# Grouped attention: the rotation's half swap as a stream shuffle on VectorE, and the row maximum split into two f32r parts

## The chip, the cores and the metric

The program runs on one core of one Trainium2 chip. The metric is the device time of one execution in microseconds (us), the median of several. In the names of the profile PE is TensorE, PEld its weight loads, DVE VectorE, ACT ScalarE, POOL GpSimd, and SP the engine whose queue issues most DMAs.

## The reference, cut to what matters

A decoder of two layers in six stages, each followed by a layer norm: grouped attention, cross attention, a gated feed forward part with attention, squared attention, another cross attention, and a mixture of experts. The change is in the first stage alone, which has 16 sequences of 128 tokens, model width 512, 32 query heads and 8 key heads of width 16:

```
q = (x @ Wq), k = (x @ Wk), v = (x @ Wv), by heads of 16 channels
rope(x) = [x1 * cos - x2 * sin, x2 * cos + x1 * sin]     # x1, x2: the two halves of a head's 16 channels
scores = q k^T / 4, causal; attn = softmax(scores); out = (attn v) Wo + b; x = layernorm(x + out)
```

The same stage of the kernel also computes what the second stage needs: its rotated queries (from the new x), its rotated keys and its values (from ctx).

## The kernel before, in words

`grouped_attention` (from line 1224) works on 16 batches b. Queries and keys are made for four batches at a time as 5 blocks of 128 channels by 512 tokens (`project(k)`, 12 f32r matmuls: three products of high and low parts, line 1470). Seven blocks are made ahead of the loop over b (`project` 0 to 6, with `project_v(0)` after block 4); the loop makes one block per batch for b + 1 = 1, 2, 3, 5, 6, 7, 9, 10, 11, two for b + 1 = 4 and 8, and none from 12 on (`blocks_of`). In three batches it also makes values (`project_v`). Beside them the loop makes one key tile (`project_key(b)`), one value tile (`project_next_v(b)`) and, from b = 2, one query tile (`project_query(b - 2)`) of the next stage.

Every tile that is rotated, 20 blocks, 16 keys and 16 queries, goes the same way. ACT copies it from PSUM to one of three buffers `raw` (`take`, lines 1691 to 1696). POOL multiplies it by the cosine (`times_cos`). PE multiplies it by a permutation matrix that swaps the halves of each head (`turn`, line 1508, f32, 128x128 by 128x512) into the PSUM tile `turn_ps`. DVE multiplies that by the sine (`times_sin`, lines 1804 and 1809). POOL adds both products (`rotate`, line 1963).

The softmax is computed on transposed scores, so the row maximum has to be turned first. For batch b the order on PE is: `scores(b, 0)`, `scores(b, 1)` (a mask matmul in bf16 and the score matmuls in f32 over four row groups), DVE's `row_max` of each half, `transpose_max(b)` (line 1553), then DVE's `split_max(b)`: the negated maximum is written to SBUF (line 1832) and cut into three bf16 parts in five instructions (lines 1832 to 1840). SP's `send_max(b)` sends the parts in three DMAs to rows of `m_row`, which has two buffers. PE goes on with `scores_t(b, 0)`, which may overwrite the PSUM tile of the turned maximum once line 1832 has read it, then `project_key(b)`, `turn` of a query, `project_next_v(b)`, and `add_max(b, 0)` (line 1575: four bf16 matmuls of 3 rows, each in its row group, which add the maximum to the scores). After that come `project_o(b - 1, 0)` (line 1607), `scores_t(b, 1)`, `add_max(b, 1)`, `project_o(b - 1, 1)`, the blocks, `scores(b + 1, ...)`, `values(b)`, `sums(b)` and so on. ACT takes the exponentials after each `add_max`.

Each engine runs its own list in the order written, and waits on semaphores that count the steps of the others. DVE's order in batch b is `normalize(b - 1)` (a reciprocal of 128x512, line 1847, and a product, line 1852), `add_v_bias(b)`, sine of a query, `residual`, `moments`, `row_max(b + 1, 0)`, `finish_norm`, sine of a key, sines of blocks but the last, `row_max(b + 1, 1)`, sine of the last block, `split_max(b + 1)`. The stages are separated by a barrier of all engines.

Of the kernel before, what the change touches and what calls it, by code (L numbers as in the profile page):

```python
# [12 lines left out]
P = 128  # L13
# [1210 lines left out]
def grouped_attention(nc, tag, x_in, x_t_in, x_out, wq_d, wk_d, wv_d, wo_d, bo_d, perm_d, cos_d, sin_d, parity_d,  # L1224
# [7 lines left out]
    AT_FIRST = BLOCKS + 2  # L1232
    with Phase(nc) as ph:
# [7 lines left out]
        perm = sb(f"{tag}_perm", [P, P])  # L1241
# [9 lines left out]
        ones_bf = sb(f"{tag}_ones_bf", [P, P], BF16)  # L1251
# [11 lines left out]
        m_neg = sb(f"{tag}_m_neg", [KV * I, P])  # L1263
        m_rest = sb(f"{tag}_m_rest", [KV * I, P])
        m_parts = sb(f"{tag}_m_parts", [KV * I, 3, P], BF16)
        m_row = sb(f"{tag}_m_row", [P, 2, 2, N], BF16)
# [23 lines left out]
        turn_ps = ph.ps(f"{tag}_turn", [P, N])  # L1290
# [13 lines left out]
        names = ("zeroed set_done w_hi_done w_lo_done x_hi_done x_lo_first x_lo_done qk_full raw_done turn_full cos_done "  # L1304
# [3 lines left out]
        (zeroed, set_done, w_hi_done, w_lo_done, x_hi_done, x_lo_first, x_lo_done, qk_full, raw_done, turn_full, cos_done,  # L1308
# [4 lines left out]
        consts = [(perm, perm_d), (cos, cos_d[:, KEY]), (sin, sin_d[:, KEY]), (parity, parity_d), (ident, ident_d),  # L1313
# [46 lines left out]
        with nc.Block() as block:  # L1360
            @block.sync
            def _(sp):
# [12 lines left out]
                def send_max(b):  # L1375
                    sp.wait_ge(m_step, 5 * (b + 1))
                    if b >= 2:
                        sp.wait_ge(st_full, 8 * (b - 1))
                    for p in range(3):
                        sp.dma_start(m_row[p:P:32, b % 2, :, :].rearrange("j h t -> j (h t)"), m_parts[:, p, :]  # L1380
                                     ).then_inc(m_ld, 16)
# [65 lines left out]
            def _(pe):  # L1447
# [107 lines left out]
                def scores_t(b, half):  # L1555

                    for j in range(4):
                        if half == 1:
                            pe.wait_ge(exp_done, 8 * b + j + 1)
                        elif j == 0:  # L1560
                            pe.wait_ge(m_step, 5 * b + 1)
                        nc.tensor.matmul(sc_ps[:, j, :].rearrange("p (i s) -> p i s", i=4), ident_bf[:, :],
                                         mask_t[:, :].rearrange("p (o s) -> p o s", o=1).to_broadcast([P, 4, P]),
                                         start=True, stop=False, skip_group_check=True)
                    for j in range(4):
                        r = slice(32 * j, 32 * j + 32)
# [46 lines left out]
                for k in range(1, BLOCKS):  # L1613
                    project(k)
                    turn(0, k - 1)
                project_v(0)
                turn(0, BLOCKS - 1)
# [5 lines left out]
                turn(0, first)  # L1623
                project(second)
                transpose_max(0)
                turn(0, second)

                for b in range(B):
# [3 lines left out]
                    if b >= 3:  # L1632
                        turn(1, b - 3)
# [15 lines left out]
                    turn(2, b)  # L1649
                    for k in blocks[-1:]:  # L1650
                        project(k)
                    for k in blocks[:-1]:
                        turn(0, k)
# [3 lines left out]
                    for k in blocks[-1:]:  # L1657
                        turn(0, k)
# [4 lines left out]
                turn(1, B - 3)  # L1663
# [3 lines left out]
                turn(1, B - 2)  # L1667
                project_query(B - 1)
                turn(1, B - 1)

            @block.scalar
            def _(act):
# [109 lines left out]
            def _(dve):  # L1782
                nc.vector.memset(ones_bf[:, :], 1.0).then_inc(set_done, 1)
# [14 lines left out]
                def times_sin(kind, n):  # L1798
                    s = at(kind, n)
                    dve.wait_ge(turn_full, s + 1)  # L1800
                    if s >= 2:
                        dve.wait_ge(rope_done, s - 1)
                    if kind == 0:
                        nc.vector.tensor_tensor(turned_s[:, s % 2, :].rearrange("p (n t) -> p n t", n=4),
                                                turn_ps[:, :].rearrange("p (n t) -> p n t", n=4),
                                                sin[:, :].rearrange("p (o t) -> p o t", o=1).to_broadcast([P, 4, P]),
                                                ALU.mult).then_inc(sin_done, 1)
# [20 lines left out]
                def split_max(b):  # L1828
                    dve.wait_ge(mT_full, b + 1)
                    if b > 0:  # L1830
                        dve.wait_ge(m_ld, 48 * b)
                    nc.vector.tensor_scalar(m_neg[:, :], sc_ps[0:KV * I, 0, 0:P], -1.0, None, ALU.mult).then_inc(m_step, 1)
                    dve.wait_ge(m_step, b * 5 + 1)
                    nc.vector.tensor_copy(m_parts[:, 0, :], m_neg[:, :]).then_inc(m_step, 1)
                    dve.wait_ge(m_step, b * 5 + 2)
                    nc.vector.tensor_tensor(m_rest[:, :], m_neg[:, :], m_parts[:, 0, :], ALU.subtract).then_inc(m_step, 1)
                    dve.wait_ge(m_step, b * 5 + 3)
                    nc.vector.tensor_copy(m_parts[:, 1, :], m_rest[:, :]).then_inc(m_step, 1)
                    dve.wait_ge(m_step, b * 5 + 4)
                    nc.vector.tensor_tensor(m_parts[:, 2, :], m_rest[:, :], m_parts[:, 1, :], ALU.subtract  # L1840
                                            ).then_inc(m_step, 1)
# [2077 lines left out]
def decoder(nc, i, out):  # L3919

    def dram(name, shape, dt=F32):
# [8 lines left out]
                      i["rope_perm"], i["a0_cos"], i["a0_sin"], i["a0_parity"], i["ident"], i["half"], i["ident_bf"],  # L3930
# [122 lines left out]
```

## Time and profile before

| | |
|---|---|
| median of 3 runs | 3454.83 us (3448.98 to 3464.68) |
| the profiled execution | 3458.54 us, its span 3456.8 us |
| mean granted TensorE clock | 0.939 of full speed |
| PE busy | 3040.2 us (88%) |
| DVE busy | 2114.3 us (61%) |
| first stage | from 0 to about 510.7 us of the span |

The span runs from the first to the last instruction of the profiled execution. "busy" is the time in which the engine had an instruction in work. PE's matmuls are pipelined and their ends are modelled, so that what a matmul takes from PE is read from the start of the next one, not from its own length. A bracket behind a row of the timeline is the idle time before it, and what ended it.

### The profile page before, as it was taken

The numbers are of one execution on the slowest core, as the hardware profiler recorded it, in microseconds if no ns is written. First come the engines' busy times: TensorE is split into PE (matmuls) and PEld (weight loads), VectorE is DVE, ScalarE is ACT, GpSimd is POOL, SyncE is SP. The second block draws the span as 40 slices with busy tenths as digits, with TensorE's granted clock in tenths as the row PEclk, the third lists the DMA queues.
The fourth block names the chain that finished last, engine by engine and source line by source line (L and its number), as shares of the span: only waits on it lengthen the run. The fifth ranks groups of instructions, "written<-read, shape, count | busy, mean of one in ns | idle before, by whom it ended". The sixth has DMA issues, their size and how long they took to land. (4 is left out here: it accounts for less than half of the span.)

```text
span 3456.8 us, 57813 instructions
## 1 busy us (share of the span) xinstructions
PE 3040.2 (88%) x21948; PEld 1766.5 (51%) x21948; DVE 2114.3 (61%) x2636; ACT 1531.2 (44%) x2642; POOL 938.5 (27%) x1397
## 2 busy tenths in 40 slices
PE   7999968999669968999996999599999995889997
PEld 4444323333256646888885676222222223767785
DVE  4555658999335443444444344699999992562167
ACT  3222324777533213333331333179999994321132
POOL 3444451333200001111120245423333331001154
PEclk9999986999879988999998999789999997899998
DMA  3222335555231005455443122323333323339976
GB/s 114 67 73 75 87 96 130 155 157 146 77 107 33 9 26 146 126 160 154 127 152 99 54 89 76 117 72 94 97 99 100 93 81 102 90 113 364 401 244 181
DMA packets 370294, 413.27 MB, mean 120 GB/s; under 512 B 62737, under 2 KB 246673, under 8 KB 368786
## 3 DMA queue, kind: packets, MB, share of 16 engines
q1 hardware_dynamic: 211552, 251.69, 23.6%
q10 hardware_dynamic: 135938, 100.69, 9.5%
q0 software_dynamic: 22528, 57.19, 5.5%
q8 instruction: 175, 2.87, 0.4%
q14 instruction: 101, 0.83, 0.1%
HBM read 299.88 MB, written 108.92 MB: 118 GB/s over the span
## 5 line engine op out<-in xcount | busy, mean ns | idle before, releaser
L394 ACT ACTIVATE c_probs<-c_st 128x512 f32<-128x512 f32 x1536 | 834.7, 597 | 214.9 <-PE c_st L320 202.6
L433 DVE TENSOR_REDUCE c_maxes<-c_s 128x2 f32<-128x1024 f32 x768 | 898.7, 1211 | 27.6 <-PE c_s L301 26.2
L337 PE MATMUL c_o<-c_probs,c_v_aug 128*32 128x256 f32 x6144 | 496.9, 395 | 46.8 <-ACT c_o_raw L404 28.9
L301 PE MATMUL c_s<-c_k_st,c_q_st 48*128 48x512 bf16 (+1 forms) x1536 | 344.8, 446 | 67.8 <-DMA c_k_st<-c_k_dram 40.1
L320 PE MATMUL c_st<-c_q_st,c_k_st 51*128 51x512 bf16 (+1 forms) x1536 | 319.6, 394 | 5.3 <-DVE c_y L459 5.1
L301 PEld LDWEIGHTS c_s<-c_k_st,c_q_st 48*128 48x128 bf16 (+1 forms) x1536 | 100.9, 128 | 401.8 <-issue 226.7
L337 PEld LDWEIGHTS c_o<-c_probs,c_v_aug 128*32 128x32 f32 x6144 | 124.4, 108 | 317.7 <-issue 214.3
L2961 DVE TENSOR_TENSOR f_w_lo<-f_w_raw,f_w_hi 128x1536 fp32r<-128x1536 f32 x64 | 116.8, 1825 | 108.7 <-ACT f_w_hi L2882 108.6
L320 PEld LDWEIGHTS c_st<-c_q_st,c_k_st 51*128 51x128 bf16 (+1 forms) x1536 | 144.0, 127 | 53.7 <-issue 23.0
L2882 ACT ACTIVATE f_w_hi<-f_w_raw 128x1536 fp32r<-128x1536 f32 x64 | 95.3, 1488 | 92.7 <-PE f_out_ps L2832 58.8
L3028 POOL CAST f_parts<-f_ctx 128x512 bf16<-128x512 f32 x16 | 12.4, 775 | 444.7 <-DMA f_ctx<-in_ctx 444.7
L2995 DVE TENSOR_TENSOR f_hidden<-f_gate,f_up_ps 128x512 f32<-128x512 f32 x64 | 43.9, 686 | 135.9 <-PE f_up_ps L2794 106.3
L1824 DVE TENSOR_REDUCE a_maxes<-a_sc 128x4 f32<-128x512 f32 x128 | 79.5, 684 | 73.6 <-PE a_sc L1544 73.6
L2589 POOL TENSOR_TENSOR a_kept<-a_weights,a_keep_t 128x512 f32<-128x512 f32 x64 | 80.4, 1289 | 142.7 <-ACT a_weights L2390 142.7
L605 POOL CAST c_m_parts<-c_m_t 128x64 bf16<-128x64 f32 (+1 forms) x96 | 23.4, 244 | 322.6 <-DVE c_m_t L443 322.6
L1148 DVE TENSOR_REDUCE g_maxes<-g_sc 128x4 f32<-128x512 f32 x64 | 39.7, 682 | 107.0 <-PE g_sc L920 107.0
L3902 POOL DMA_INDIRECT f_early<-x_dram,f_e_token x22 | 20.9, 952 | 301.2 <-PE f_up_ps L3318 211.5
L2918 ACT ACTIVATE f_hidden_hi<-f_hidden 128x512 fp32r<-128x512 f32 x64 | 40.5, 632 | 140.4 <-DVE f_hidden L2995 140.4
L1734 ACT ACTIVATE a_probs<-a_sc 128x512 f32<-128x512 f32 x128 | 66.1, 602 | 82.2 <-PE a_sc L1575 82.2
L2832 PE MATMUL f_out_ps<-f_w_hi,f_hidden_hi 128*128 128x512 f32 x256 | 99.7, 389 | 0.0
L2832 PE MATMUL f_out_ps<-f_w_lo,f_hidden_hi 128*128 128x512 f32 x256 | 99.6, 389 | 0.0
L2832 PE MATMUL f_out_ps<-f_w_hi,f_hidden_lo 128*128 128x512 f32 x256 | 99.6, 389 | 0.0
(419 smaller groups left out, 6017.7 us busy)
## 6 DMA issues: line engine op xcount, KB each, us to landing
f_w_raw<-in_f_win ACTq DMA_DIRECT2D x96, 256.0 KB, 3.1
f_w_raw<-in_f_wup ACTq DMA_DIRECT2D x96, 256.0 KB, 3.4
f_w_raw<-in_f_wdown ACTq DMA_DIRECT2D x96, 256.0 KB, 3.7
c_o_dram<-c_o_raw SPq DMA_DIRECT2D x64, 256.0 KB, 2.5
f_x<-x_dram SPq DMA_DIRECT2D x48, 256.0 KB, 4.3
c_k_dram<-f_parts ACTq DMA_DIRECT2D x96, 128.0 KB, 2.7
c_q_dram<-a_parts SPq DMA_DIRECT2D x96, 128.0 KB, 2.4
c_q_st<-c_q_dram SPq DMA_DIRECT2D x128, 96.0 KB, 2.2
```

The source lines that it names most:

```text
L301: mm = nc.tensor.matmul(s1_ps[:, i, half, :], q_st[r:r + ROWS, s, i, tt * P:(tt + 1) * P], k_st[r:r + ROWS, s, i, :], start=True, stop=True)
L320: nc.tensor.matmul(st_ps[:, st_bank(j, e), :], k_st[r:r + ROWS + MP, s, i, st * P:(st + 1) * P], q_st[r:r + ROWS + MP, s, i, :], start=Tru ...
L337: mm = nc.tensor.matmul(o_ps[32 * h:32 * h + 32, queries], v_aug[:, (j // NG) % NBS, st, head_of(j, h), :], probs[:, (st * 4 + i * 2 + hal ...
L394: nc.scalar.activation(probs[:, e % 8, :], st_ps[:, st_bank(j, e), :], ACT.Exp).then_inc(exp_done, 1)
L433: nc.vector.tensor_reduce(maxes[:, j % 2, :].rearrange("p (h r) -> p h r", h=2)[:, :, i * KT + tt], s1_ps[:, i, :, :], AX.X, ALU.max).then ...
L1734: nc.scalar.activation(probs[:, half, j, :], sc_ps[:, j, :], ACT.Exp).then_inc(exp_done, 1)
L1824: nc.vector.tensor_reduce(out[:, 2 * half:2 * half + 2, :], sc_ps[:, j, :].rearrange("p (i h s) -> p i h s", i=2, h=2), AX.X, ALU.max).the ...
L2589: nc.gpsimd.tensor_tensor(kept[:, b % 2, j, :, :], weights[:, j, :, :], keep_t[:, :].rearrange("p (o s) -> p o s", o=1).to_broadcast([P, D ...
L2832: mm = nc.tensor.matmul(out_ps[:, t, :], a[:, f % 2, tokens], w[:, n % RING, DOWN, :], start=(f == 0 and k == 0), stop=(f == NF - 1 and k ...
L2882: nc.scalar.activation(w_hi[:, n % RING, :, :], w_raw[:, n % 2, :, :], ACT.Copy).then_inc(w_hi_done, 1)
L2961: nc.vector.tensor_tensor(w_lo[:, n % RING, :, :], w_raw[:, n % 2, :, :], w_hi[:, n % RING, :, :], ALU.subtract).then_inc(w_lo_done, 1)
L2995: nc.vector.tensor_tensor(hidden[:, f % 2, :], gate[:, f % 2, :], up_ps[:, f % 2, :], ALU.mult).then_inc(hidden_done, 1)
```

## The change

The rotation: `turn`, its PSUM tile, its semaphore and the permutation matrix (a DMA of 64 KB among the constants) are gone. DVE swaps the halves itself, by a stream shuffle inside each group of 32 partitions, from `raw` to `turned_s`, and multiplies `turned_s` by the sine in place. The wait for the constants moves to PE's list ahead of the first scores. The maximum: two parts in f32r instead of three in bf16, both read from PSUM, so that `split_max` has two instructions; two DMAs instead of three, of twice the bytes each; one buffer of `m_row` instead of two. `scores_t(b, 0)` now waits for both instructions of `split_max`, and the matmuls of `add_max` have two f32r rows. Cut to its core:

```diff
+    SWAP = [c - c % 16 + (c % 16 + 8) % 16 for c in range(32)]
-        m_parts = sb(f"{tag}_m_parts", [KV * I, 3, P], BF16)
-        m_row = sb(f"{tag}_m_row", [P, 2, 2, N], BF16)
+        m_parts = sb(f"{tag}_m_parts", [KV * I, 2, P], F32R)
+        m_row = sb(f"{tag}_m_row", [P, 2, N], F32R)
                 def send_max(b):
-                    sp.wait_ge(m_step, 5 * (b + 1))
-                    if b >= 2:
-                        sp.wait_ge(st_full, 8 * (b - 1))
-                    for p in range(3):
+                    sp.wait_ge(m_step, 2 * (b + 1))
+                    if b > 0:
+                        sp.wait_ge(st_full, 8 * b)
+                    for p in range(2):
...
-                def turn(kind, n):
-                    s = at(kind, n)
-                    pe.wait_ge(raw_done, s + 1)
-                    if s == 0:
-                        pe.wait_ge(const_ld, 16 * NCONST)
-                    else:
-                        pe.wait_ge(sin_done, s)
-                    nc.tensor.matmul(turn_ps[:, :], perm[:, :], raw[:, s % RAWS, :], start=True, stop=True
-                                     ).then_inc(turn_full, 1)
                 def scores_t(b, half):
-                            pe.wait_ge(m_step, 5 * b + 1)
+                            pe.wait_ge(m_step, 2 * (b + 1))
                 def add_max(b, half):
-                        nc.tensor.matmul(sc_ps[:, j, :], ones_bf[32 * j:32 * j + 3, :],
-                                         m_row[32 * j:32 * j + 3, b % 2, half, :],
+                        nc.tensor.matmul(sc_ps[:, j, :], ones_r[32 * j:32 * j + 2, :],
+                                         m_row[32 * j:32 * j + 2, half, :],
...
                 def take(kind, n):
                     if s >= RAWS:
-                        act.wait_ge(turn_full, s - RAWS + 1)
+                        act.wait_ge(swapped, s - RAWS + 1)
                 def times_sin(kind, n):
                     s = at(kind, n)
-                    dve.wait_ge(turn_full, s + 1)
+                    out = turned_s[:, s % 2, :]
+                    dve.wait_ge(raw_done, s + 1)
                     if s >= 2:
                         dve.wait_ge(rope_done, s - 1)
+                    nc.vector.stream_shuffle(out, raw[:, s % RAWS, :], SWAP).then_inc(swapped, 1)
+                    dve.wait_ge(swapped, s + 1)
-                        nc.vector.tensor_tensor(turned_s[:, s % 2, :], turn_ps[:, :], next_sin[:, :], ALU.mult
-                                                ).then_inc(sin_done, 1)
+                        nc.vector.tensor_tensor(out, out, next_sin[:, :], ALU.mult).then_inc(sin_done, 1)
                 def split_max(b):
-                    nc.vector.tensor_scalar(m_neg[:, :], sc_ps[0:KV * I, 0, 0:P], -1.0, None, ALU.mult).then_inc(m_step, 1)
-                    nc.vector.tensor_copy(m_parts[:, 0, :], m_neg[:, :]).then_inc(m_step, 1)
-                    nc.vector.tensor_tensor(m_rest[:, :], m_neg[:, :], m_parts[:, 0, :], ALU.subtract).then_inc(m_step, 1)
-                    nc.vector.tensor_copy(m_parts[:, 1, :], m_rest[:, :]).then_inc(m_step, 1)
-                    nc.vector.tensor_tensor(m_parts[:, 2, :], m_rest[:, :], m_parts[:, 1, :], ALU.subtract
-                                            ).then_inc(m_step, 1)
+                    turned = sc_ps[0:KV * I, 0, 0:P]
+                    nc.vector.tensor_scalar(m_parts[:, 0, :], turned, -1.0, None, ALU.mult).then_inc(m_step, 1)
+                    dve.wait_ge(m_step, b * 2 + 1)
+                    nc.vector.scalar_tensor_tensor(out=m_parts[:, 1, :], in0=turned, scalar=-1.0, in1=m_parts[:, 0, :],
+                                                   op0=ALU.mult, op1=ALU.subtract).then_inc(m_step, 1)
```

All calls of `turn` in PE's list are taken out: four between the first projections, one after `project_v(0)`, two more ahead of the loop, and in each batch one after `values`, one after `project_key` (from b = 3), and one for each block, of which the last stands after `sums`. At the end of the stage there are three more, for the last queries.

## Rows read from the trace of the kernel before

**Rows 1.** Windows over the first stage, then the timeline of PE where the second begins.

```profile
50.30:510.70 460.40, 407.81 (x2302) 177.45 (x2300) 261.01 (x372) 121.65 (x224) 194.33 (x164) 0.96 0.26 76
...
516.81 0.80 PE L301 MATMUL c_s<-c_k_st,c_q_st 48*128 48x512 f32 x2 [19.14 <-DMA c_k_st<-c_k_dram]
```

**Rows 2.** Timeline of PE: batch 7's wait (first row), then batch 8.

```profile
263.74 0.39 PE L1575 MATMUL a_sc<-a_m_row,a_ones_bf 3*128 3x512 bf16 x4 [1.57 <-DMA a_m_row<-a_m_parts]
...
289.71 1.04 PE L1562 MATMUL a_sc<-a_mask_t,a_ident_bf 128*128 128x512 bf16 x4 [0.37 <-DVE a_m_neg L1832]
...
293.65 1.16 PE L1497 MATMUL a_proj<-a_next_wv,a_ctx 128*128 128x128 f32 x8
295.40 0.39 PE L1575 MATMUL a_sc<-a_m_row,a_ones_bf 3*128 3x512 bf16 x4 [0.59 <-DMA a_m_row<-a_m_parts]
296.47 1.98 PE L1607 MATMUL a_misc<-a_wo,a_o_norm 128*128 128x512 f32 x4 [0.68 <-DVE a_o_norm L1852]
...
313.88 1.12 PE L1508 MATMUL a_turn<-a_raw,a_perm 128*128 128x512 f32 x2
314.84 1.02 PE L1490 MATMUL a_proj<-a_x_new,a_next_wq 128*128 128x512 f32 x2
...
316.34 1.04 PE L1562 MATMUL a_sc<-a_mask_t,a_ident_bf 128*128 128x512 bf16 x4 [0.37 <-DVE a_m_neg L1832]
```

**Rows 3.** Timeline of PE: batch 13, which has no block.

```profile
418.73 1.04 PE L1562 MATMUL a_sc<-a_mask_t,a_ident_bf 128*128 128x512 bf16 x4 [0.37 <-DVE a_m_neg L1832]
...
424.80 1.98 PE L1607 MATMUL a_misc<-a_wo,a_o_norm 128*128 128x512 f32 x4 [0.65 <-DVE a_o_norm L1852]
...
434.57 1.12 PE L1508 MATMUL a_turn<-a_raw,a_perm 128*128 128x512 f32 x2
```

**Rows 4.** Timeline of DVE: the end of batch 8; the last row is of batch 13.

```profile
312.18 2.48 DVE L1824 TENSOR_REDUCE a_maxes<-a_sc 128x4 f32<-128x512 f32 x4 [4.08 <-PE a_sc L1544]
315.04 0.69 DVE L1804 TENSOR_TENSOR a_turned_s<-a_turn,a_sin 128x512 f32<-128x512 f32 x1 [0.38 <-PE a_turn L1508]
316.01 0.28 DVE L1832 TENSOR_SCALAR a_m_neg<-a_sc 32x128 f32<-32x128 f32 x1 [0.28 <-PE a_sc L1553]
316.32 0.88 DVE L1834 CAST a_m_parts<-a_m_neg 32x128 bf16<-32x128 f32 x1
317.24 1.25 DVE L1836 TENSOR_TENSOR a_m_rest<-a_m_neg,a_m_parts 32x128 f32<-32x128 f32 x1
...
318.98 3.34 DVE L1847 RECIPROCAL a_recip<-a_misc 128x512 f32<-128x512 f32 x1
...
437.73 2.48 DVE L1824 TENSOR_REDUCE a_maxes<-a_sc 128x4 f32<-128x512 f32 x4 [1.30 <-PE a_sc L1544]
```

**Rows 5.** Single lines of DVE, count, ns least/median/most.

```profile
L1863 DVE BATCH_NORM_STATS2 a_stats<-a_y x16: 694/695/695, 88.6 to 488.9; 128x6 f32<-128x512 f32 x16
...
L1874 DVE TENSOR_SCALAR a_x_new<-a_y,a_mv,a_rstd x16: 534/536/1492, 95.9 to 490.7; 128x512 f32<-128x512 f32 x16
...
L1836 DVE TENSOR_TENSOR a_m_rest<-a_m_neg,a_m_parts x16: 279/1252/1316, 49.5 to 463.6; 32x128 f32<-32x128 f32 x16
```

**Rows 6.** Timeline of PE in the second stage: two f32r matmuls in two row groups.

```profile
700.19 0.40 PE L320 MATMUL c_st<-c_q_st,c_k_st 50*128 50x512 f32 x2
```

**Rows 7.** Timelines of ACT, PE and DVE ahead of the loop.

```profile
26.22 0.60 ACT L1691 ACTIVATE a_raw<-a_proj 128x512 f32<-128x512 f32 x1
...
30.50 3.73 PE L1523 MATMUL a_proj<-a_wv,a_x_t 128*128 128x128 f32 x32
...
39.88 1.19 PE L1470 MATMUL a_proj<-a_x_hi,a_w_hi 128*128 128x512 f32 x4
...
48.82 0.28 DVE L1832 TENSOR_SCALAR a_m_neg<-a_sc 32x128 f32<-32x128 f32 x1 [0.86 <-PE a_sc L1553]
```

**Rows 8.** Windows of the four stretches of the stage at a lower clock.

```profile
199.80:206.65 6.85, 6.61 (x16) 2.38 (x20) 1.38 (x3) 2.17 (x5) 2.51 (x2) 0.53 0.61 170
...
sum 20.52, PE 19.86 PEld 7.19 DVE 4.08 ACT 6.68 POOL 9.03; mean PE 4.97 PEld 1.80 DVE 1.02 ACT 1.67 POOL 2.26
```

More of the change, by code:

```diff
@@ L1250, in grouped_attention @@
         ones_pad = sb(f"{tag}_ones_pad", [P, 2, 32])
-        ones_bf = sb(f"{tag}_ones_bf", [P, P], BF16)
+        ones_r = sb(f"{tag}_ones_r", [P, P], F32R)
         x_t = sb(f"{tag}_x_t", [P, 2, DK, N])
@@ L1303, in grouped_attention @@
         next_v_stored = sem(f"{tag}_next_v_stored")
-        names = ("zeroed set_done w_hi_done w_lo_done x_hi_done x_lo_first x_lo_done qk_full raw_done turn_full cos_done "
+        names = ("zeroed set_done w_hi_done w_lo_done x_hi_done x_lo_first x_lo_done qk_full raw_done swapped cos_done "
                  "sin_done rope_done pad_done v_full v_done s1_full max_done mT_full m_step m_ld st_full exp_done o_full "
@@ L1312, in grouped_attention @@
              sem(f"{tag}_{n}") for n in names]
-        consts = [(perm, perm_d), (cos, cos_d[:, KEY]), (sin, sin_d[:, KEY]), (parity, parity_d), (ident, ident_d),
+        consts = [(cos, cos_d[:, KEY]), (sin, sin_d[:, KEY]), (parity, parity_d), (ident, ident_d),
                   (ident_bf, ident_bf_d), (mask, mask_d), (mask_t, mask_t_d), (minus_half, half_d), (bo, bo_d),
@@ L1375, in send_max @@
                 def send_max(b):
-                    sp.wait_ge(m_step, 5 * (b + 1))
-                    if b >= 2:
-                        sp.wait_ge(st_full, 8 * (b - 1))
-                    for p in range(3):
-                        sp.dma_start(m_row[p:P:32, b % 2, :, :].rearrange("j h t -> j (h t)"), m_parts[:, p, :]
-                                     ).then_inc(m_ld, 16)
+                    sp.wait_ge(m_step, 2 * (b + 1))
+                    if b > 0:
+                        sp.wait_ge(st_full, 8 * b)
+                    for p in range(2):
+                        sp.dma_start(m_row[p:P:32, :, :].rearrange("j h t -> j (h t)").bitcast(F32),
+                                     m_parts[:, p, :].bitcast(F32)).then_inc(m_ld, 16)
                 def store(b):
@@ L1614, in _ @@
                     project(k)
-                    turn(0, k - 1)
                 project_v(0)
-                turn(0, BLOCKS - 1)
+                pe.wait_ge(const_ld, 16 * NCONST)
                 pe.wait_ge(set_done, 5)
@@ L1622, in _ @@
                 scores(0, 1)
-                turn(0, first)
                 project(second)
                 transpose_max(0)
-                turn(0, second)
                 for b in range(B):
@@ L1631, in _ @@
                     project_key(b)
-                    if b >= 3:
-                        turn(1, b - 3)
                     project_next_v(b)
@@ L1648, in _ @@
                     values(b)
-                    turn(2, b)
                     for k in blocks[-1:]:
                         project(k)
-                    for k in blocks[:-1]:
-                        turn(0, k)
                     if b + 1 < B:
@@ L1656, in _ @@
                     sums(b)
-                    for k in blocks[-1:]:
-                        turn(0, k)
                     if b >= 2:
@@ L1662, in _ @@
                         transpose_max(b + 1)
-                turn(1, B - 3)
                 project_query(B - 2)
@@ L1666, in _ @@
                 project_o(B - 1, 1)
-                turn(1, B - 2)
                 project_query(B - 1)
-                turn(1, B - 1)
             @block.scalar
@@ L1782, in _ @@
             def _(dve):
-                nc.vector.memset(ones_bf[:, :], 1.0).then_inc(set_done, 1)
+                nc.vector.memset(ones_r[:, :].bitcast(F32), 1.0).then_inc(set_done, 1)
                 for half in range(2):
@@ L3929, in decoder @@
     grouped_attention(nc, "a0", i["x"], i["x_t"], x1, i["a0_wq"], i["a0_wk"], i["a0_wv"], i["a0_wo"], i["a0_bo"],
-                      i["rope_perm"], i["a0_cos"], i["a0_sin"], i["a0_parity"], i["ident"], i["half"], i["ident_bf"],
+                      i["a0_cos"], i["a0_sin"], i["a0_parity"], i["ident"], i["half"], i["ident_bf"],
                       i["mask"], i["mask_t"], i["ctx"], [i["c0_wq"], i["c0_wk"], i["c0_wv"]], i["c0_bqk"], i["c0_bv"],
@@ L4039 @@
         a[f"c0_{name}"] = np.concatenate([t / 4, t], 1)
-    a["rope_perm"] = np.zeros((P, P), np.float32)
-    a["rope_perm"][c - c % 16 + (c % 16 + 8) % 16, c] = 1
     nc = _bacc.Bacc("TRN2", target_bir_lowering=False, num_devices=1)
```

20 lines of the change are left out of this document (6 added, 14 removed).

## The prediction

> **What bounds the kernel now.** I read the windows first: the loop of the first stage is 460.40 us, PE is busy for 407.81 of them (89%) and DVE for 261.01 (57%) [rows 1]. The second stage's first matmul has waited 19.14 us for data that the first stage stores [rows 1], so the stages run one after the other and what the first one gains is kept. Then I read PE's timeline. PE works almost without a gap from `project_o` to `transpose_max`; its idle time lies in three places of each batch: 0.37 us for the first instruction of `split_max`, 0.59 us (batch 8) or 1.57 us (batch 7) for the DMA of the maximum, 0.68 us for DVE's `o_norm` [rows 2]. The last two hang on DVE: `split_max` takes from 316.01 to 318.98, only then does the reciprocal of 3.34 us start, and the product after it [rows 4]. So PE bounds most of a batch, and DVE the piece between the turned maximum and `project_o`.
>
> **First part of a batch, from `scores_t` to `project_o`.** The two instructions that stay in `split_max` take 0.28 us each; the second now has to end before `scores_t` starts, with 0.03 us between them: 0.31 us later for PE. From there `project_next_v` starts 3.94 us after `scores_t` (293.65 - 289.71), and this stays although the turn between them goes: PE must wait for ACT's copy of the key tile anyway. `project_next_v` takes 1.09 us of PE (to 294.74, where it then waits) and `add_max` 0.39 less its overlap, 0.33. So `project_o` can start 0.31 + 3.94 + 1.09 + 0.33 = 5.67 us after the old start of `scores_t`, if data and `o_norm` are there. They are: the parts are ready some 2.4 us earlier (318.98 - 316.32, less 0.31) with one DMA fewer to issue, and the reciprocal starts as much earlier, so that `o_norm` is ready 0.6 + 3.34 + 0.7 = 4.6 us after the start of `split_max` [rows 4]. Before, it started after 6.76 us in batch 8 [rows 2]: gain 1.09. Batch 7's DMA wait is 0.98 longer (1.57 against 0.59): gain 2.05. Batch 13 took 424.80 - 418.73 = 6.07 [rows 3]: gain 0.40. The timeline puts batches 3 to 7 with batch 7, 8 to 11 with 8, and 13 to 15 with 13; I count 1 and 2 as 8, and 12 as 13. Batch 0 has no `project_o` but loses a turn ahead of it, 0.85. Sum: 5 x 2.05 + 6 x 1.09 + 4 x 0.40 + 0.85 = **19.2 us**.
>
> **Second part, to the next `split_max`.** A turn takes 0.96 us of PE (314.84 - 313.88) [rows 2]. In the 9 batches with one block, the turn after `values` is simply gained, 0.97. The one after `sums` is not: DVE's list is the limit there. Before, the last row maximum ended at 314.66 and the next `split_max` began at 316.01, 1.35 us later [rows 4]. Now the block's shuffle and sine must fit between: 2 x 0.69 + 0.05 = 1.43. Gain 0.97 - 0.08 = 0.89 each, 8.0 us. The 2 batches with two blocks also gain the first block's turn, 0.86: 1.75 each, 3.5 us. In the 4 batches without a block only the turn after `values` goes, and there DVE stands close: it had 1.30 us of idle time before the second row maximum [rows 4], PE would come 0.97 + 0.40 earlier while a shuffle of 0.69 is added, so that half is given back: 0.5 each, 2.0 us. Sum: **13.5 us**.
>
> **What a shuffle costs.** The trace has none. By rows it lies between 0.54 us, a one-input operation of the same 128x512 tile, and the reciprocal's 3.34 us; the nearest is the statistics operation, which reads one such SBUF tile in 0.695 us [rows 4, 5]. I take 0.69, and 0.06 more for setting up the permutation, on the 20 shuffles that lie on a path that sets the end (15 at the ends of batches, 3 ahead of the loop, 2 in the tail): -1.2 us. The other 32 lie in DVE's idle time: 4.08 us before the row maximum of batch 8 [rows 4]. Less than nothing it can't be. Here the Trainium skill speaks against the change: "VectorE: DVE Perf Modes", the perf-mode tier table, gives the shuffle about 2.4 us for 2048 elements, with one element per cycle only; as an estimate from that figure at the page's 0.96 GHz, 512 elements are 0.8 us. By it the 20 shuffles would cost 1 us more than I charge, and the sum hardly changes.
>
> **`add_max` in f32r.** Four bf16 matmuls in four row groups run side by side, 0.39 us for all [rows 2]. If four f32r ones ran one behind the other it would be 3 x 0.21 more, 32 times: -20 us. Against this stands the second stage, where two f32r matmuls in two row groups take 0.40 together [rows 6], as one would. I charge 0.05 each for the longer weight load: -1.6 us; bounds 0 and -20. The single `m_row` buffer costs nothing: `send_max(b)` waits for `add_max(b - 1, 1)`, which in PE's list stands ahead of all that the next maximum is made from.
>
> **Ahead of the loop.** Four turns go from between the projections, where `project_v(0)` started at 30.50. It needs ACT's fourth `raw` tile, ready at 26.8 [rows 7]: 3.6 us earlier. `project(5)` then moves from 39.88 to about 32.7. The next limit is DVE: two blocks in a row with shuffle and sine, the sines held up by POOL's cosine; the second scores start at 37.8 rather than 42.8, and the block after them adds a shuffle. I get the first `split_max` at 43.7 instead of 48.82 [rows 7]: **5.1 us**, bounds 3 and 6.5. **Tail:** after the last batch DVE has two shuffles more before the last reciprocal's product and the query tile whose stores end the stage: -1.4 us.
>
> **The clock.** In four stretches, 20.52 us together, the granted clock is at 1.2 instead of 2.4 GHz (the first row's 0.53 is the mean over a window that it nearly fills) [rows 8]; they begin inside `project_o` of batches 4 to 7, right behind the waits of 1.57 and 0.7 us. A PE that is busy all through such a stretch loses half of it, 10.3; by its gaps I take 9.0 us. With both waits gone I expect the stretches to go: **+9.0**, bounds 0 and 10, and below 0 if the new idle time (1.2 us ahead of `scores_t`, 0.9 us ahead of `project_next_v`) brings new ones.
>
> **Sum:** 19.2 + 13.5 + 5.1 - 1.4 - 1.2 - 1.6 + 9.0 = 42.6 us off the profiled execution's 3458.5: 3415.9. The median of the runs before is 3.7 us below that execution; put on it, the same gain gives 3412. I forecast between them, **3414 us**.
>
> **Rivals.** (1) The waits go but the clock still falls in as many stretches: PE's idle time is moved, not removed. For it: 2.1 us of new idle time in a batch. Against: batches 1 to 3 wait like that and keep the full clock. Gain 33.6: 3421 to 3425. (2) DVE becomes the limit by its port with POOL. The line of `split_max` that reads two SBUF tiles takes 0.28 us at best and 1.25 in the median, with POOL's cosine or sum beside it [rows 5]; the sine now reads two SBUF tiles too, before it read PSUM. If POOL is at work at the end of each batch, 15 times up to 0.57 us more (1.27 of a POOL product less the 0.70 that the shuffle has covered), 8.6 us, and as much again if sines in the middle of a batch push the row maxima: 3423 to 3431. Against: POOL's cosine of the last block ends before the last row maximum does. The Trainium skill has this as a rule ("SBUF — State Buffer", who interferes with whom: whichever of a VectorE operation with two SBUF inputs and a reading GpSimd operation starts second is blocked); the trace agrees by that line. (3) Four f32r matmuls run in sequence: gain 22.6, and the clock's share may stay: 3432 to 3440. (4) Slower: the shuffle is as dear as the reciprocal. It lies on the path at the end of every batch, 3.34 less 0.75 us more 20 times, -52: 3466, and 3475 when the longer wait keeps the clock low. It decides from 2.9 us per shuffle on (0.75 + 42.6 / 20). Nothing in the rows but the upper bound speaks for it. (5) The change does less than it says, because ACT's or SP's lists hold PE where the turns stood: then only the first part and the clock are left, 28 us, 3428.
>
> **Numbers.** Chances: forecast 0.58 (3405 to 3420), (1) 0.15, (2) 0.10, (3) 0.05, (4) 0.04, (5) 0.08. 0.5% is 17 us, about what this measurement can tell from no change. Faster by more (below 3437.6): all but (4), half of (3) and some of (2) and (5): 0.87; within 0.5%, these and the lower end of (4): 0.10; slower, the rest of (4): 0.03. The range has to reach to (2) and (5): 3402 to 3436; its lower end is the sum with all the clock and 6.5 us ahead of the loop, on a fast run.
>
> **What would show it.** No wait for `m_row` or `o_norm` in PE's timeline, `project_o` about 5.3 us behind `scores_t`; batches with a block shorter by some 2 us (3.9 where batch 7's wait was); an idle of 1 to 1.5 us ahead of `scores_t`, ended by DVE; shuffles of 0.7 to 0.8 us; `add_max` at 0.4 us; the first stage ended at about 468 us instead of 510.7; the other stages unchanged. A shuffle above 1.3 us, `add_max` near 1 us, or more time at 1.2 GHz in the first stage would make it wrong.

## The result and the profile after

The kernel after takes 3418.22 us in the median of 4 runs (3416.38 to 3421.04), the kernel before 3455.44 in runs on the same chip. The ratio is 0.988, 95% interval 0.986 to 0.9905. The profiled execution took 3416.38 us, its span 3414.6: 42.2 us less than that of before.

First where the time went. These are windows of the kernel after: the loop up to the barrier, and all behind it. The columns are those of [rows 1]: length, busy time of PE, PEld, DVE, ACT, POOL, then granted clock, DMA share, GB/s.

```profile
44.60:470.80 426.20, 366.86 (x2211) 162.60 (x2211) 256.36 (x415) 121.87 (x224) 195.80 (x165) 0.96 0.28 82
470.80:3414.60 2943.80, 2594.18 (x19475) 1563.87 (x19476) 1836.69 (x2229) 1394.18 (x2392) 722.36 (x1215) 0.94 0.41 126
```

The same window behind the barrier, of the kernel before:

```profile
510.70:3456.80 2946.10, 2596.01 (x19476) 1563.34 (x19476) 1833.13 (x2229) 1394.25 (x2392) 725.26 (x1215) 0.94 0.41 126
```

The first stage is 39.9 us shorter (510.7 to 470.8), the five others together 2.3 us, which is scatter: their code is the same. Inside the loop PE lost 407.81 - 366.86 = 41 us of busy time, but the loop became only 34.2 us shorter (460.40 to 426.20); PE is idle for 59.3 us of it where it was for 52.6. Work taken off PE is therefore no measure of the gain: swap_only (below) takes the same turns out and gains nothing.

PE's timeline after, batch 8; it answers to [rows 2]. The last row is the start of batch 9.

```profile
257.84 1.04 PE L1549 MATMUL a_sc<-a_mask_t,a_ident_bf 128*128 128x512 bf16 x4 [1.48 <-DVE a_m_parts L1811]
...
259.88 1.13 PE L1478 MATMUL a_proj<-a_ctx,a_next_wk 128*128 128x512 f32 x2
261.78 1.16 PE L1494 MATMUL a_proj<-a_next_wv,a_ctx 128*128 128x128 f32 x8 [0.78 <-ACT a_raw L1670]
262.87 0.51 PE L1562 MATMUL a_sc<-a_m_row,a_ones_r 2*128 2x512 f32 x4
263.31 1.98 PE L1594 MATMUL a_misc<-a_wo,a_o_norm 128*128 128x512 f32 x4
...
282.58 1.04 PE L1549 MATMUL a_sc<-a_mask_t,a_ident_bf 128*128 128x512 bf16 x4 [1.48 <-DVE a_m_parts L1811]
```

The waits for `m_row` and `o_norm` are gone. Two stand in their place: 1.48 us ahead of `scores_t` (0.37 before), ended by `split_max`, and 0.78 ahead of `project_next_v`, ended by ACT's key tile. `project_o` stands 5.47 us behind `scores_t` (6.76 before), and batch 8 lasts 24.74 us (26.63).

DVE's timeline after, the end of the same batch; it answers to [rows 4].

```profile
278.17 2.49 DVE L1800 TENSOR_REDUCE a_maxes<-a_sc 128x4 f32<-128x512 f32 x4 [2.44 <-PE a_sc L1531]
280.57 0.01 DVE L1778 LOAD_MASK_SELECT a_turned_s<-a_raw  x1
280.57 0.72 DVE L1778 STREAM_SHUFFLE a_turned_s<-a_raw 128x512 f32<-128x512 f32 x1
281.33 0.69 DVE L1781 TENSOR_TENSOR a_turned_s<-a_turned_s,a_sin 128x512 f32<-128x512 f32 x1
281.94 0.27 DVE L1809 TENSOR_SCALAR a_m_parts<-a_sc 32x128 fp32r<-32x128 f32 x1
282.24 0.28 DVE L1811 SCALAR_TENSOR_TENSOR a_m_parts<-a_sc,a_m_parts 32x128 fp32r<-32x128 f32 x1
282.45 3.33 DVE L1818 RECIPROCAL a_recip<-a_misc 128x512 f32<-128x512 f32 x1
```

From the last row maximum to `split_max` DVE does not pause: shuffle and sine take 1.37 us of it, while PE, done with `transpose_max` (280.83), stands still. And single lines of DVE after, to set beside [rows 5] (count, ns least/median/most):

```profile
L1778 DVE STREAM_SHUFFLE a_turned_s<-a_raw x52: 710/724/745, 20.7 to 456.1; 128x512 f32<-128x512 f32 x52
L1786 DVE TENSOR_TENSOR a_turned_s<-a_turned_s,a_next_sin x32: 691/693/1695, 60.8 to 456.9; 128x512 f32<-128x512 f32 x32
L1781 DVE TENSOR_TENSOR a_turned_s<-a_turned_s,a_sin x20: 691/694/1304, 21.5 to 334.4; 128x512 f32<-128x512 f32 x20
...
L1811 DVE SCALAR_TENSOR_TENSOR a_m_parts<-a_sc,a_m_parts x16: 278/278/279, 44.3 to 420.5; 32x128 fp32r<-32x128 f32 x16
```

### The profile page after: what moved, and what is told of

It is laid out like the page before. It is cut to its first block and busy times, and to the rows that moved or that the text cites. A ratio compares the mean times of both kernels' runs of the same rounds, so it can differ in the third digit from the quotient of the medians.

```text
span 3414.6 us, 57593 instructions
## 1 busy us (share of the span) xinstructions
PE 2991.2 (88%) x21843; PEld 1749.2 (51%) x21844; DVE 2118.2 (62%) x2692; ACT 1531.2 (45%) x2642; POOL 935.6 (27%) x1397
## 5 line engine op out<-in xcount | busy, mean ns | idle before, releaser
L433 DVE TENSOR_REDUCE c_maxes<-c_s 128x2 f32<-128x1024 f32 x768 | 898.9, 1211 | 24.0 <-PE c_s L301 22.6
L301 PE MATMUL c_s<-c_k_st,c_q_st 48*128 48x512 bf16 (+1 forms) x1536 | 343.5, 444 | 70.4 <-DMA c_k_st<-c_k_dram 42.6
L605 POOL CAST c_m_parts<-c_m_t 128x64 bf16<-128x64 f32 (+1 forms) x96 | 23.4, 244 | 319.7 <-DVE c_m_t L443 319.6
L2885 ACT ACTIVATE f_gate<-f_gate_ps 128x512 f32<-128x512 f32 x64 | 38.2, 597 | 115.0 <-PE f_gate_ps L2786 59.0
```

What stands on the lines that cost most here:

```text
L301: mm = nc.tensor.matmul(s1_ps[:, i, half, :], q_st[r:r + ROWS, s, i, tt * P:(tt + 1) * P], k_st[r:r + ROWS, s, i, :], start=True, stop=True)
L433: nc.vector.tensor_reduce(maxes[:, j % 2, :].rearrange("p (h r) -> p h r", h=2)[:, :, i * KT + tt], s1_ps[:, i, :, :], AX.X, ALU.max).then ...
```

## The experiments

The edits' own effect is read where the second stage's first matmul starts. Medians of whole runs move more: that of the kernel before was 3455.44 to 3461.93 us from one set of runs to another. But each start comes from one profiled execution, and a fall of the clock ahead of batch 1, which some executions have, moves it by 1.5 to 2.4 us (clock_fill, own_fill below), in max_only by 3.6. Before it starts at 516.8, after at 476.9 (6 us behind the barrier). One batch with one block, batch 9, is cut into three pieces from PE's timelines: from `project_o(7)` to `transpose_max(9)`, from there to `scores_t(9)`, from there to `project_o(8)`.

| kernel | second stage starts | to transpose | to scores_t | to project_o | ratio to before (95%) |
|---|---|---|---|---|---|
| before | 516.8 | 19.23 | 0.65 | 6.76 | |
| swap_only | 519.1 | 19.15 | 1.44 | 7.12 | 0.999 (0.996 to 1.002) |
| swap_fill | 503.5 | 17.53 | 1.44 | 7.13 | 0.995 (0.992 to 0.997) |
| max_only | 493.4 | 19.23 | 0.96 | 5.47 | 0.993 (0.990 to 0.995) |
| after | 476.9 | 17.52 | 1.75 | 5.47 | 0.988 (0.986 to 0.991) |
| last_twice | 494.8 | 17.52 | 2.38 | 5.46 | 0.994 (0.991 to 0.997) |
| middle_twice | 480.6 | 17.53 | 1.76 | 5.46 | 0.988 (0.983 to 0.992) |
| clock_fill | 473.0 | 17.53 | 1.76 | 5.47 | 0.986 (0.982 to 0.990) |
| early_split | 464.2 | 17.52 | 0.96 | 5.46 | 0.984 (0.978 to 0.990) |
| early_own | 445.9 | 17.51 | 0.96 | 4.42 | 0.980 (0.976 to 0.985) |
| own_fill | 447.3 | 17.51 | 0.96 | 4.42 | 0.980 (0.977 to 0.982) |

### Each edit alone: swap_only and max_only

swap_only has the hunks of the diff for `times_sin`, `turn` and `swapped`, max_only those for `m_parts`, `m_row` and `ones_r`.

> The kernel before with the rotation by stream shuffle alone; the row maximum stays in five steps and three bf16 parts. My theory: the turns leave TensorE, but in the first part of a batch the wait for m_row takes their place, because the chain split, DMA, add_max is as long as before and starts no earlier relative to scores_t. So the second part (13.5 us by my sum), some 3 us ahead of the loop and little else: first stage ends near 492 (510.7 before, 470.8 with both edits), TensorE still waits for m_row in every batch, the granted clock still falls inside the stage behind such waits, time about 3437 us. Rival (the edits are independent, each giving what is its own): the first part shrinks here too by the 13 turns taken out of it, 0.86 us each, the stage ends near 481 and the time is near 3426. Rival (the DVE is the limit from here on): five split steps behind a shuffle hold scores_t as long as in the changed kernel, idle ahead of scores_t 1.2 to 1.5 us.

> The kernel before with the maximum split into two f32r parts from PSUM, turns kept on TensorE. My theory: the wait for m_row goes, what stands between scores_t and project_o is project_key, turn, next_v and the wait for raw, about 6.3 us for 7.7 and 6.8 before: some 8 us over the batches, some 1.5 us ahead of the loop, and up to 9 us if the clock no longer falls inside the loop: stage end 492 to 501, time about 3437 to 3446. If the clock gain of the changed kernel belongs to the shorter idle times of the maximum, no fall between 150 and 280 us is seen here; if it belongs to the turns being gone, the four falls stay and the stage ends near 500. Rival (f32r add_max in sequence): add_max pairs take 1.6 us longer per batch and this kernel is slower than before.

swap_only gained nothing: its stage is 2.3 us longer, which one such fall would explain, though all 52 turns of 0.96 us left PE, 42 of them in the loop. Its timeline of PE in batch 9:

```profile
310.48 1.04 PE L1551 MATMUL a_sc<-a_mask_t,a_ident_bf 128*128 128x512 bf16 x4 [1.17 <-DVE a_m_neg L1810]
...
314.42 1.16 PE L1496 MATMUL a_proj<-a_next_wv,a_ctx 128*128 128x128 f32 x8 [0.78 <-ACT a_raw L1672]
316.54 0.39 PE L1564 MATMUL a_sc<-a_m_row,a_ones_bf 3*128 3x512 bf16 x4 [0.96 <-DMA a_m_row<-a_m_parts]
317.60 3.15 PE L1596 MATMUL a_misc<-a_wo,a_o_norm 128*128 128x512 f32 x4 [0.67 <-DVE a_o_norm L1830]
320.54 1.60 PE L1551 MATMUL a_sc<-a_mask_t,a_ident_bf 128*128 128x512 bf16 x4
```

Four waits of 3.6 us together, from 309.3 to 317.6; then `project_o` takes 3.15 us for 1.98 ([rows 2]). The window over its loop has a granted clock of 0.93:

```profile
50.00:500.00 450.00, 383.67 (x2189) 163.51 (x2189) 294.43 (x458) 120.59 (x222) 189.84 (x161) 0.93 0.25 75
```

At two levels (1.2 and 2.4 GHz) that is 0.07 x 2 x 450 = 63 us at the lower one. The same window of the kernel before has 0.97 (0.03 x 2 x 450 = 27: the four stretches of [rows 8] have 20.5, the rest lies behind 485, at the end of the stage), that of max_only, up to 470, 0.99:

```profile
50.00:500.00 450.00, 408.11 (x2303) 177.45 (x2300) 261.31 (x372) 121.02 (x223) 193.37 (x163) 0.97 0.26 75
```

```profile
50.00:470.00 420.00, 399.69 (x2307) 178.92 (x2306) 223.76 (x326) 120.43 (x222) 191.51 (x161) 0.99 0.27 80
```

I had expected swap_only some 20 us better: I had charged its clock with what the kernel before loses, not with what its own new idle time brings on. max_only did better than expected (493.4 - 6 = 487 for 492 to 501). From batch 3 on its only wait between `transpose_max` and `project_o` is 0.69 us ahead of `scores_t` (batches 1 and 2 have 1.17 and 0.78), and its clock stays up from batch 1 to the last batch, with all turns still on PE. So the clock's share came with the shorter chain of the maximum. Alone the edits give -2.3 and 23.4 us, together 39.9: they don't add. The turns are worth nothing by themselves, and 16.5 us (493.4 to 476.9) once the maximum is short; of these, 3.6 are a loss of max_only alone, whose clock falls ahead of batch 1 (`transpose_max(1)` at 77.18, 73.54 before).

### Is it the clock? swap_fill

```
 project_key(b)
+fill(1)                    # 128x512 f32 matmul into a spare bank
 project_next_v(b)
+fill(1)
 ...
 transpose_max(b + 1)
+fill(1)
```

> The kernel with the shuffle alone, and three spare 128x512 f32 matmuls into a bank that nobody reads in each batch, 0.96 us each, put where TensorE idles: behind transpose_max (idle 1.17 us), behind project_key (0.78 us) and behind project_next_v (0.96 us of waiting for m_row). They add work and take no wait away. Theory (the shuffle alone gave nothing because TensorE idles three to four times in a row around scores_t and its clock then falls: 15 times and 61 us at half clock before the stage's end, 20 us in the kernel before, whose 20.5 us cost 9.0): with the idle time filled the clock stays up, and the stage ends 20 to 27 us earlier, first matmul of the next stage at 492 to 499 for 519.1, time about 3430 us. Rival (the clock falls for another reason than TensorE's idle time, or the lost time lies in the waits themselves): stage end 519 or up to 8 us later, by 45 fillers that overrun their gaps by 0.18 us.

The stage is 15.6 us shorter than in swap_only, with 47 matmuls more and the same time from `scores_t` to `project_o` (7.13). The whole difference is in the piece behind, 17.53 for 19.15 us. PE's rows of batch 9, then the window over the loop:

```profile
301.12 1.04 PE L1557 MATMUL a_sc<-a_mask_t,a_ident_bf 128*128 128x512 bf16 x4 [0.31 <-DVE a_m_neg L1819]
...
306.05 1.02 PE L1543 MATMUL a_spare<-a_next_cos,a_ident 128*128 128x512 f32 x2
307.18 0.39 PE L1570 MATMUL a_sc<-a_m_row,a_ones_bf 3*128 3x512 bf16 x4
308.24 1.98 PE L1602 MATMUL a_misc<-a_wo,a_o_norm 128*128 128x512 f32 x4 [0.67 <-DVE a_o_norm L1839]
```

```profile
50.00:460.00 410.00, 389.60 (x2254) 168.29 (x2257) 280.05 (x438) 116.72 (x216) 176.24 (x149) 0.98 0.26 77
```

`project_o` is back at 1.98 us, the clock at 0.98. The fillers add work and take no wait away, so this shows that the clock fell for PE's idle time, and that the lower clock ate what the removed turns had given. The size was below my 20 to 27 us. Some falls stayed (0.02 x 2 x 410 = 16 us); that I had also priced them too high is likely, but not shown by itself. From 519.1 to 503.5 is the clock; from 503.5 to 476.9 (26.6 us) are the waits for the maximum, with the clock falls that remained.

Idle time alone does not decide it, though. In batch 1 the kernel before has four waits just like those shown for swap_only, 3.3 us together, and `project_o` still runs at full clock (the window 74.60:84.00 has 1.00):

```profile
74.67 1.04 PE L1562 MATMUL a_sc<-a_mask_t,a_ident_bf 128*128 128x512 bf16 x4 [0.86 <-DVE a_m_neg L1832]
...
80.68 0.39 PE L1575 MATMUL a_sc<-a_m_row,a_ones_bf 3*128 3x512 bf16 x4 [0.91 <-DMA a_m_row<-a_m_parts]
81.81 1.98 PE L1607 MATMUL a_misc<-a_wo,a_o_norm 128*128 128x512 f32 x4 [0.74 <-DVE a_o_norm L1852]
```

What tells such a batch from one that loses the clock, no run here shows.

### DVE ahead of split_max: early_split, last_twice, middle_twice

```
# early_split, VectorE's list
 normalize(b - 1)
+times_sin(0, last block of blocks_of(b))
 add_v_bias(b)
 ...
 row_max(b + 1, 1)
-times_sin(0, last block of blocks_of(b + 1))
 split_max(b + 1)
# and split_max(0) ahead of times_sin(0, first)
# last_twice (last block of a batch), middle_twice (keys and queries)
+nc.vector.stream_shuffle(dump, raw[:, s % RAWS, :], SWAP)
 nc.vector.stream_shuffle(out, raw[:, s % RAWS, :], SWAP)
```

> The changed kernel with VectorE's order altered: split_max(b+1) stands right behind row_max(b+1,1), and the shuffle and sine of the last block of blocks_of(b+1) move to the next batch, behind normalize. Theory (VectorE's shuffle and sine ahead of split_max bound scores_t in the 11 batches with a block): idle of TensorE ahead of scores_t falls from 1.48 to about 0.7 us in these batches, 8 to 9 us off the stage (end near 462 for 470.8), and the clock falls at 68.8 and 99.5 may go with the idle time (up to 3 us more): about 3408 us. Rival (the time returns elsewhere): the moved shuffle and sine hold add_v_bias, row_max or the q_t of the next block, project_o comes 1.5 us later behind scores_t, and the stage ends where it did: 3416 to 3420 us.

> The changed kernel with a second, idle shuffle (into a buffer that nobody reads) ahead of the shuffle of the last block of a batch, 11 in all. If VectorE in front of split_max bounds scores_t there, each costs its own duration and a semaphore step, 0.73 to 0.8 us: +8 to +9 us, stage end near 479.5, idle ahead of scores_t 2.2 us for 1.48. If TensorE alone is the limit (the idle time being the transpose's own latency), nearly nothing: 0 to 2 us.

> The changed kernel with a second, idle shuffle ahead of that of each key and query of the next attention (kinds 1 and 2, 32 in all, 29 of them inside the loop), 0.79 us each. Theory (these stand in front of row_max(b+1,0) and row_max(b+1,1), with slack behind TensorE's work): nothing in the block batches, whose bound is what follows row_max(b+1,1); the last three, behind the loop, are on VectorE's and GpSimd's path to the end: +1 to +2.4 us. Stage end 477 to 480. Rival (VectorE is full from normalize to split_max and each shuffle there costs its time, as the one ahead of split_max does): 29 x 0.79 = 23 us more, stage end near 500.

One row for each, the same `scores_t(9)`: early_split, last_twice, middle_twice.

```profile
272.47 1.04 PE L1549 MATMUL a_sc<-a_mask_t,a_ident_bf 128*128 128x512 bf16 x4 [0.69 <-DVE a_m_parts L1811]
```

```profile
296.27 1.04 PE L1551 MATMUL a_sc<-a_mask_t,a_ident_bf 128*128 128x512 bf16 x4 [2.11 <-DVE a_m_parts L1816]
```

```profile
282.75 1.04 PE L1551 MATMUL a_sc<-a_mask_t,a_ident_bf 128*128 128x512 bf16 x4 [1.48 <-DVE a_m_parts L1818]
```

The idle time of 1.48 us is DVE's list. With the shuffle and sine out of the way it is 0.69; with one spare shuffle more there, 2.11; with a spare shuffle elsewhere, 1.48. early_split gained 12.7 us where I expected 8 to 9 and up to 3: 11 x 0.79 = 8.7, and the falls in batches 1 and 2, 1.6 each, are gone. last_twice lost 17.9 where I expected 8 to 9: 11 x 0.63 = 6.9 is the idle time, and in 9 of the 11 batches with a block `project_o` now stands 7.0 to 7.1 us behind `scores_t` instead of 5.47, against 2 in the kernel after: 7 x 1.6 = 11.2. So 0.63 us more of idle time cost more by the clock than by itself; that part of last_twice I had missed. middle_twice lost 3.7: at most 0.12 in a batch with a block, 0.64 in each of the four without (batch 14: 21.29 to 21.93), the rest behind the loop. The rival, a DVE that is full everywhere, would have cost 23 us.

### The falls that are left: clock_fill

```
 transpose_max(b + 1)
+fill(1)                    # b = 0, 1 only
 ...
 project_query(B - 2)
+fill(3)
 project_o(B - 1, 0)
```

> The changed kernel with spare 128x512 matmuls: one behind transpose_max(1) and transpose_max(2), in the idle 1.59 us ahead of scores_t, and three ahead of project_o(15), in the idle 3.07 us. Theory: the half clock at 68.8 and 99.5 and at 440.9 follows this idle time. With it filled, project_o stands 5.5 us behind scores_t in batches 1 and 2 too (7.08 now), the last project_o takes 3.7 us for 6.5, and the stage ends 4 to 6 us earlier (476.9 to 471 to 473). Rival: the clock falls there for what comes before (stage start, the empty place of project_query in batches 0 and 1) and not for the idle time: 476.9 stays, or is 0.5 us later.

In the kernel after, the clock falls right at `scores_t` of batches 1 and 2 (PE's timeline, then the window of the first fall):

```profile
66.89 0.28 PE L1540 MATMUL a_sc<-a_ident,a_maxes 128*32 128x128 f32 x1 [0.70 <-DVE a_maxes L1800]
68.76 1.89 PE L1549 MATMUL a_sc<-a_mask_t,a_ident_bf 128*128 128x512 bf16 x4 [1.59 <-DVE a_m_parts L1811]
70.58 1.91 PE L1554 MATMUL a_sc<-a_q_t,a_k_pad 32*128 32x512 f32 x8
```

```profile
68.80:72.20 3.40, 3.40 (x12) 0.91 (x12) 3.37 (x2) 0.00 (x0) 2.04 (x2) 0.50 0.20 57
```

These batches have no `project_query` between `sums` and `transpose_max`, so that PE idles twice there, 0.70 and 1.59 us; later batches idle 1.48 and keep the clock. clock_fill, the same batch:

```profile
68.50 1.02 PE L1541 MATMUL a_spare<-a_next_cos,a_ident 128*128 128x512 f32 x2
70.26 1.04 PE L1555 MATMUL a_sc<-a_mask_t,a_ident_bf 128*128 128x512 bf16 x4 [0.74 <-DVE a_m_parts L1820]
...
75.73 1.98 PE L1600 MATMUL a_misc<-a_wo,a_o_norm 128*128 128x512 f32 x4
```

`scores_t` takes 1.04 us for 1.89, and the last `project_o` 3.70 us (the kernel after took 6.52). The stage is 3.9 us shorter; 1.6 each is from the two batches and 2.2 from the end. 1.5 us went again at the stage's beginning, which is the same code in both kernels (a later first `scores_t`, a fall in batch 0).

### A version that beats both: early_own and own_fill

The turns left a PSUM bank free. early_own is early_split with `next_v` in it:

```
-pe.wait_ge(raw_done, at(2, n) + 1)
-matmul(proj_ps[:, i * P:(i + 1) * P], ctx[...], next_wv)
+matmul(next_v_ps[:, i * P:(i + 1) * P], ctx[...], next_wv)
```

> The version with the split early, and next_v's projection in the bank that the turns left free instead of proj_ps, so that it no longer waits for ScalarE's copy of the key (0.77 us in each of 16 batches). If add_max then still finds m_row there and project_o still finds o_norm (done at 252.45, project_o would start at 253.2 in batch 8), the whole goes: -12 us, first matmul of the next stage at 452 for 464.2, time about 3391 us. If the wait moves to m_row, as it did with the shuffle alone, less than 3 us are won.

> The version with the split early and next_v in its own bank, and three spare 128x512 matmuls (2.74 us) ahead of the last project_o, where TensorE idles 3.06 us and the last project_o then takes 5.18 us, partly at half clock. If the clock holds, project_o(15) takes 3.70 us: 1.5 us off the stage, first matmul of the next stage at 444.4 for 445.9, time 3387 us, which the medians cannot tell from 3388.6. Rival: nothing, 445.9.

PE's timeline of early_own, batch 9:

```profile
261.81 1.04 PE L1549 MATMUL a_sc<-a_mask_t,a_ident_bf 128*128 128x512 bf16 x4 [0.69 <-DVE a_m_parts L1811]
...
263.85 1.12 PE L1479 MATMUL a_proj<-a_ctx,a_next_wk 128*128 128x512 f32 x2
264.81 1.05 PE L1494 MATMUL a_next_v_ps<-a_next_wv,a_ctx 128*128 128x128 f32 x8
265.80 0.51 PE L1562 MATMUL a_sc<-a_m_row,a_ones_r 2*128 2x512 f32 x4
266.24 1.98 PE L1594 MATMUL a_misc<-a_wo,a_o_norm 128*128 128x512 f32 x4
```

A batch is 1.05 us shorter, not 0.78: from `project_key` to `project_next_v` it is 0.96 us, with the wait it was 261.78 - 259.88 = 1.90 (0.94 of the 1.05), so ending the wait gave 0.16 us more than the 0.78 that the profile calls idle. I had expected 452; the second stage starts at 445.9, 31 us ahead of the kernel after, and no wait moved to `m_row`; the median is 3388.57 us (3386.52 to 3403.11), ratio 0.980. own_fill did what it was to do at the end of the stage (`project_o` 3.70 us, 1.0 us gained) but had a clock fall in batch 0, in code that both share (`transpose_max(1)` at 67.44, in early_own 65.06), so that the stage ended at 447.3 and not at the 444.4 expected; the medians (3388.70 and 3388.57) don't tell them apart.

## Why the prediction was right

Forecast 3414, measured 3418.2; forecast gain of one execution 42.6 us, measured 42.2. Of these 2.3 lie behind the first stage and are luck; the stage itself gave 39.9. From `scores_t(0)` to `scores_t(15)` the gain is 36.8 us (50.32 to 463.34 before, 44.59 to 420.81 after); without the clock's part (9.0 less 3.2, below) it is 31.0, where the steps for the loop add up to 19.2 + 13.5 - 1.6 - 0.9 (15 shuffles) = 30.2. By the steps:

- **First part of a batch.** Forecast: `project_o` 5.67 us behind the old start of `scores_t`. Measured 5.47 + 0.31 = 5.78. By groups of batches the gain is 7.72 - 5.78 = 1.94 (2.05 forecast), 6.76 - 5.78 = 0.98 (1.09), 6.07 - 5.78 = 0.29 (0.40). The 0.11 is `add_max` in f32r, which the prediction had charged apart. Batches 1 and 2 gained nothing: `project_o` stands 7.08 and 7.05 us behind `scores_t` (7.14 before), and `scores_t` comes later, for there the clock fell.
- **Second part.** Forecast 0.89 per batch with one block. Measured 19.23 - 17.52 = 1.71 for the two turns, less 1.75 - 0.65 - 0.31 = 0.79 of new idle time: 0.92. With two blocks, 1.75 forecast and 22.84 - 20.30 - 0.79 = 1.75 measured (from batch 3 to batch 4); without a block, 0.5 forecast and 15.59 - 14.85 = 0.74 measured. The reason given, DVE's list as the limit, is what early_split and last_twice showed.
- **Ahead of the loop.** `split_max(0)` at 43.95, forecast 43.7 (48.82 before [rows 7]).
- **Shuffle.** 0.724 us and 0.01 for the mask, forecast 0.69 and 0.06. The estimate from the Trainium skill ("VectorE: DVE Perf Modes", perf-mode tier table) was 0.8; the shuffle's 0.724 stands between the two, and with the mask's 0.01 it is what the prediction charged, 0.75, within 0.02. Hiding the others was right but for the batches without a block: middle_twice cost 0.64 in each of these.
- **Port.** The sine product reads two SBUF tiles. 42 of the 52 ran with no POOL operation beside them, among them the last of all 11 batches that make a block, and took 0.69 us. The other ten met POOL's cosine or sum: six up to batch 0, one each in the two batches with two blocks, two at the end. They took 0.75 to 1.70 us, each ending some 0.55 us behind POOL's operation:

```profile
145.81 1.31 POOL L1934 TENSOR_TENSOR a_whole<-a_turned_c,a_turned_s 128x512 f32<-128x512 f32 x1 [2.76 <-DVE a_turned_s L1786]
146.37 1.30 DVE L1781 TENSOR_TENSOR a_turned_s<-a_turned_s,a_sin 128x512 f32<-128x512 f32 x1
```

  So the collision of rival 2 is real, and it cost little because POOL was idle where it would have counted, as the prediction had argued against it. The 1.25 us line [rows 5] is gone: its successor reads PSUM and one SBUF tile and takes 278 to 279 ns in all 16, in 12 of them with POOL's sum at work beside it. The Trainium skill's rule ("SBUF — State Buffer", who interferes with whom) is about two SBUF inputs, and both lines agree with it.
- **f32r.** The first `add_max` takes PE 0.44 us (262.87 to 263.31) for 0.33 (385.67 to 386.00 in swap_fill, where nothing waits), side by side in four row groups. About what was charged; rival 3 is out. (Its gain should have read 24.2 us and not 22.6: the 20 us stand in place of the 1.6 already charged.)
- **Tail.** 2.6 us instead of 1.4: from `scores_t(15)` to the barrier 50.0 us, before 47.4. The last `project_o` follows 3.07 us of idle time and runs at the lower clock:

```profile
441.94 6.52 PE L1594 MATMUL a_misc<-a_wo,a_o_norm 128*128 128x512 f32 x8 [3.07 <-DVE a_o_norm L1823]
453.33 2.05 PE L1487 MATMUL a_proj<-a_x_new,a_next_wq 128*128 128x512 f32 x2 [4.87 <-DVE a_x_new L1845]
476.85 0.80 PE L301 MATMUL c_s<-c_k_st,c_q_st 48*128 48x512 f32 x2 [21.47 <-DMA c_k_st<-c_k_dram]
```

- **Clock.** The four stretches of [rows 8] are gone, and the 9.0 us charged for them was right: from `project_o` to the next `transpose_max` they had 20.85, 25.81, 22.21 and 24.26 us, where max_only, with the same turns at full clock, has 19.23, 22.81, 19.22 and 22.85, 9.0 less in all. Two new ones of 3.4 us, in batches 1 and 2, took some 3.2 back. Against rival 1 stood that batches 1 to 3 wait like that and keep the clock; batches 1 and 2 kept it before, with 1.13 us from transpose to `scores_t`, and not with 1.87.

What the number doesn't show is that the steps hold only together. The prediction gave the second part and the piece ahead of the loop, 18.6 us, to the turns. On top of the shorter maximum that is about right: 18.6 less 1.4 for the tail and 1.2 for the shuffle is 16.0, and the turns gave 16.5, less the 3.6 that max_only lost by itself ahead of batch 1, plus the 3.2 of the new falls, 16.1. By themselves the turns gave -2.3 us. The prediction had named the danger (new idle time may bring new falls) and bounded the clock by it, but only for both edits together. Rival 1 was the fate of the shuffle alone.

Open: how the 26.6 us between swap_fill and the kernel after divide between waits and remaining falls, why the clock falls in batch 0 in some kernels (clock_fill, own_fill) with code that doesn't differ there, and what else than idle time decides, since batches 1 and 2 of the kernel before kept the clock with 3.3 us of it, batch 3 kept it with waits of 1.57 and 0.66, and batches 4 to 7 lost it with the same two.

## What to carry to other kernels

Taking work off an engine that waits several times in a row turns work into more idle time, and on TensorE that can cost the clock for the next microseconds: shorten the wait first, or put both in one change, and read the granted clock of each single edit. Where two operations stand between an engine's last input and the small one that releases another engine, issue the small one first; here that move was worth 12.7 us, beside the 39.9 of the whole change. When a change frees a PSUM bank, look which wait exists only because two results share one.

## What the runs showed of the hardware

- Filling TensorE's idle time kept its clock up: 47 useless matmuls more made the stage 15.6 us shorter. Idle times of 1.48 us, with 0.78 some 3 us behind, kept 2.4 GHz in all nine batches that had them; 2.11 to 2.21 us in the same place brought 1.2 GHz in 9 of 11 batches, 1.6 us lost each time; so did 0.70 and 1.59 with `transpose_max` alone between them, in 2 of 2. It is no fixed rule: in the kernel before, waits of 1.57 and 0.66 us kept the clock in batch 3 and lost it in batches 4 to 7.
- VectorE's product of two SBUF tiles, begun while a GpSimd product or sum ran, ended some 0.55 us behind that (0.75 to 1.70 us, ten times) and took 0.69 us otherwise (42 times); with one operand in PSUM the small operation of `split_max` took 0.28 us beside GpSimd in 12 of 12.
- A 128x512 f32 stream shuffle takes 0.72 us, about what the statistics operation takes on the same tile (0.695 [rows 5]), and setting its mask 0.01.
- Four f32r matmuls of 2 rows in four row groups run side by side, 0.44 us for the first `add_max` of a batch, where four bf16 ones of 3 rows took 0.33 (swap_fill).
